# Layer 3's cross-attention weights loaded during layer 1's experts, and their token-free preparation moved into the head of layer 2's cross-attention

## The reference

```python
q_in = x @ Wq + (x @ q_down @ q_up) * alpha_q / 32
org_ctx, ipa_ctx = context[:, :end], context[:, end:]          # end = 12544 - 4
k_in = org_ctx @ Wk + (org_ctx @ k_down @ k_up) * alpha_k / 32
v_in = org_ctx @ Wv + (org_ctx @ v_down @ v_up) * alpha_v / 32
out = _attention(q_in, k_in, v_in)                              # 16 heads of 64
out = out + _attention(q_in, ipa_ctx @ Wk_ipa, ipa_ctx @ Wv_ipa)  # the last 4 tokens
return out @ Wo + bo + lora(out, o_down, o_up, o_alpha)
```

## Time and profile before

| | |
|---|---|
| median of 3 runs | 3099.08 us (3098.6 to 3107.48) |
| the profiled execution, own time | 3106.17 us |
| its span, first to last instruction | 3104.5 us |
| PE busy | 2802.7 us, 90% |
| DVE busy | 1799.1 us, 58% |
| mean granted TensorE clock | 0.914 of 2.4 GHz |
| x2, the streamed cross-attention of layer 2 | 1312.0 to 1641.6 us |
| L3_q, the first stage of x3 | 1741.6 to 1840.4 us |
| L_units, 112 units | from 1841.7 us |

### The profile page before, as it was taken

One profiled execution on the slowest core, in us unless ns is written; L12 is line 12 of the kernel. 1 busy time (PEld: TensorE's weight loads), 2 busy tenths in 40 slices (PEclk: granted clock), 3 DMA queues, 4 the chain that ended last, 5 costly groups with the idle time before them and its releaser, 6 DMA issues. The chain is left out here.

```text
span 3104.5 us, 65465 instructions
## 1 busy us (share of the span) xinstructions
PE 2802.7 (90%) x26651; PEld 2312.9 (75%) x26651; DVE 1799.1 (58%) x3184; ACT 1322.1 (43%) x2169; POOL 409.8 (13%) x579
## 2 busy tenths in 40 slices
PE   7999869996699984889995699999999999999968
PEld 6999837773267764747774269999999999999857
DVE  5666468884378844578863235555555555555433
ACT  4555437772067761247771004443334444443311
POOL 3444400011001000000000041202020202000000
PEclk9999979997689996979996659999999999999879
DMA  5889697656777721687736411010000100000026
GB/s 165 323 304 346 261 255 192 175 140 215 216 186 188 190 58 48 213 198 188 188 105 226 114 42 42 12 31 20 23 25 18 33 10 1 1 1 1 18 77 223
DMA packets 193632, 393.98 MB, mean 127 GB/s; under 512 B 30472, under 2 KB 161865, under 8 KB 182574
## 3 DMA queue, kind: packets, MB, share of 16 engines
q1 hardware_dynamic: 178525, 341.33, 37.9%
q10 hardware_dynamic: 14804, 48.39, 4.1%
HBM read 290.13 MB, written 99.52 MB: 126 GB/s over the span
## 5 line engine op out<-in xcount | busy, mean ns | idle before, releaser
L878 DVE TENSOR_REDUCE L_xattn_tops<-psum 128x1 f32<-128x896 f32 x672 | 704.7, 1084 | 177.2 <-PE psum L704 175.0
L801 ACT ACTIVATE L_xattn_probs<-psum 128x512 f32<-128x512 f32 x1176 | 612.7, 601 | 352.1 <-PE psum L717 349.7
L1882 DVE TENSOR_SCALAR_CACHE_REDUCE L_units_raw<-psum 128x448 f32<-128x448 f32 x448 | 277.3, 619 | 463.0 <-PE psum L1798 460.5
L1842 ACT ACTIVATE L_units_raw<-L_units_raw,L_units_negmax 128x896 f32<-128x896 f32 x224 | 221.7, 1037 | 593.2 <-DVE L_units_negmax L1892 593.2
L1818 PE MATMUL psum<-wide_tokens,L_units_high 128*128 128x386 f32 x1568 | 456.7, 358 | 1.4 <-DVE L_units_low L1901 1.4
L704 PE MATMUL psum<-L_xattn_keys,L_xattn_q_stack 96*128 96x448 bf16 (+1 forms) x1344 | 390.2, 374 | 57.6 <-DMA L_xattn_q_stack<-query_parts 22.2
L717 PEld LDWEIGHTS psum<-L_xattn_q_stack,L_xattn_keys 99*128 99x128 bf16 (+1 forms) x4704 | 308.4, 98 | 169.9 <-issue 76.8
L717 PE MATMUL psum<-L_xattn_q_stack,L_xattn_keys 99*128 99x128 bf16 (+1 forms) x4704 | 406.3, 222 | 6.0 <-POOL L_xattn_q_stack L850 2.2
L1819 PE MATMUL psum<-wide_tokens,L_units_low 128*128 128x194 f32 x1568 | 395.4, 252 | 0.0
L733 PE MATMUL psum<-L_xattn_probs,L_xattn_values 128*17 128x128 f32 x9408 | 333.6, 278 | 1.5 <-issue 1.5
L1818 PEld LDWEIGHTS psum<-wide_tokens,L_units_high 128*128 128x128 f32 x1568 | 294.7, 188 | 11.2 <-DVE L_units_low L1901 1.6
(11 more groups left out here) (497 smaller groups left out, 3737.0 us busy)
## 6 DMA issues: line engine op xcount, KB each, us to landing
key_parts<-proj_parts SPq DMA_DIRECT2D x84, 672.0 KB, 5.3
L_xattn_keys<-key_parts SPq DMA_DIRECT2D x252, 224.0 KB, 4.6
L_xattn_keys<-key_parts SPq DMA_DIRECT2D x252, 168.0 KB, 3.6
values_scratch<-held ACTq DMA_DIRECT2D x12, 1904.0 KB, 11.6
L_xattn_values<-values_scratch SPq DMA_DIRECT2D x45, 476.0 KB, 6.1
values_scratch<-proj_values ACTq DMA_DIRECT2D x9, 1904.0 KB, 9.1
L_ffn_w<-in_L_ffn_w SPq DMA_DIRECT2D x16, 1024.0 KB, 7.4
L_experts_w<-in_L_ffn_W SPq DMA_DIRECT2D x16, 1024.0 KB, 11.6
```

The source lines that it names most:

```text
L801: act.activation(group_probs(k), score_bank(k), ACT.Exp).then_inc(sem("probs"), 1)
L878: dve.tensor_reduce(tops[:, h % 2, 2 * c + w:2 * c + w + 1], top_slot(n), AX.XY, ALU.max)\
L1842: act.activation(half, half, ACT.Exp, bias=new).then_inc(sem("probs"), 1)
L1882: dve.tensor_scalar(raw[u % 2][:, s * SUB:s * SUB + width], bank(g, s % 2, 0, width), 0.0, None, ALU.add, ALU.max, accum_out=tops[:, h, s: ...
```

## The change

A new function loads six weights of layer 3 on SP at the end of f1, behind expert 7's `w2`. They go into buffers that exist from f1 on (`g.early`, `g.wv_a`, `g.wv_b`, `g.q_down`); `g.early` later serves for tiles of the last two stages as well.

```diff
+def layer3_weights(eng, g, a):
+    n, landed = "L3_xattn_", g.layer3.sem("weights")
+    eng.dma_start(g.wkT, a[n + "Wk_T"].rearrange("(i p) c -> p i c", p=128)).then_inc(landed, 16)
+    eng.dma_start(g.wv_a[:], a[n + "Wv"][0:128, :]).then_inc(landed, 16)
+    eng.dma_start(g.wv_b[:], a[n + "Wv"][128:C, :]).then_inc(landed, 16)
+    landed = g.layer3q.sem("weights")
+    eng.dma_start(g.q_down[:], a[n + "q_down"].rearrange("(k p) n -> p k n", p=128)).then_inc(landed, 16)
+    eng.dma_start(g.q_up, a[n + "q_up"]).then_inc(landed, 16)
+    eng.dma_start(g.wq3, a[n + "Wq"].rearrange("(k p) n -> p k n", p=128)).then_inc(landed, 16)
```

In `streamed_cross_attention`, for layer 2 alone (`prepares`), each engine gets work. The small operands are slices of `probs`, which is free until unit 0. On PE the first part stands behind the query's products and ahead of the wait for `stack`; the rest is called in the loop over units:

```diff
+                if prepares:
+                    pe.wait_ge(sem("low_rank"), 16 * 7)
+                    for i in range(IG):
+                        pe.matmul(bank(g, 4 + i // 2, i % 2 * C, i % 2 * C + C), k_up[:, i * 128:i * 128 + 128], k_downT,
+                                  start=True, stop=True, skip_group_check=True).then_inc(sem("wk_in_psum"), 1)
+                    for j in range(2):
+                        cols = slice(j * BANK, j * BANK + BANK)
+                        pe.matmul(bank(g, j), v_downT[:, 0:128], v_up[:, cols], start=True, stop=True)
+                        pe.matmul(bank(g, 2 + j)[0:C1, :], v_downT[:, 128:C], v_up[:, cols], start=True, stop=True)\
+                          .then_inc(sem("wv_in_psum"), 1)
+                    pe.wait_ge(sem("wv"), 4)
                 pe.wait_ge(sem("stack"), STACK)
...
                     if k == 0:
                         pe.wait_ge(sem("key_rows"), 16)
+                        if prepares:
+                            pe.wait_ge(sem("v_ipa"), 2)
...
+                def ipa_keys():
+                    pe.wait_ge(sem("ipa_loads"), 16 * 6)
+                    pe.wait_ge(sem("wk"), 4)
+                    for i in range(IG):
+                        cols, out = slice(i * 128, i * 128 + 128), bank(g, 4, i * IPA, i * IPA + IPA)
+                        pe.matmul(out, wk_ipa_a[:, cols], ipa_a, start=True, stop=False, skip_group_check=True)
+                        last = pe.matmul(out, wk_ipa_b[:, cols], ipa_b, start=False, stop=True, skip_group_check=True)
+                    last.then_inc(sem("k_ipa_in_psum"), 1)
+
+                def ipa_values(j):
+                    pe.wait_ge(sem("rep"), 2)
+                    cols, out = slice(j * BANK, j * BANK + BANK), bank(g, 5 + j)[0:H * IPA, :]
+                    pe.matmul(out, rep_a, wv_ipa_a[:, cols], start=True, stop=False)
+                    pe.matmul(out, rep_b, wv_ipa_b[:, cols], start=False, stop=True).then_inc(sem("v_ipa_in_psum"), 1)
...
                     ahead, now = v < NU, 0 <= u < NU
+                    if prepares and u == -5:
+                        ipa_keys()
+                    if prepares and u in (-4, -3):
+                        ipa_values(u + 4)
```

On ACT seven loads stand ahead of the wait for the split query, and six loads and three copies behind the first values, ahead of the exponentials:

```diff
+                    if prepares:
+                        for dst, name3 in ((k_downT, "k_down_T"), (k_up, "k_up"), (v_downT, "v_down_T"), (v_up, "v_up")):
+                            act.dma_start(dst, a[n3 + name3]).then_inc(sem("low_rank"), 16)
+                        for i, which in enumerate("qkv"):
+                            act.dma_start(g.alpha3[:, i:i + 1], row_view(a[f"{n3}{which}_alpha"], 0, 1))\
+                               .then_inc(sem("low_rank"), 16)
                     act.wait_ge(sem("qparts"), 1)
...
                     fill_values(act, 0, c, n)
+                if prepares:
+                    for dst, src in ((ipa_a, a["ctxT"][0:128, NK - IPA:NK]), (ipa_b, a["ctxT"][128:C, NK - IPA:NK]),
+                                     (wk_ipa_a, a[n3 + "Wk_ipa"][0:128, :]), (wk_ipa_b, a[n3 + "Wk_ipa"][128:C, :]),
+                                     (wv_ipa_a, a[n3 + "Wv_ipa"][0:128, :]), (wv_ipa_b, a[n3 + "Wv_ipa"][128:C, :])):
+                        act.dma_start(dst, src).then_inc(sem("ipa_loads"), 16)
+                    act.wait_ge(sem("k_ipa_in_psum"), 1)
+                    act.copy(g.k_ipa[:].rearrange("p i j -> p (i j)"), bank(g, 4, 0, IG * IPA)).then_inc(sem("k_ipa"), 1)
+                    for j in range(2):
+                        act.wait_ge(sem("v_ipa_in_psum"), j + 1)
+                        act.copy(g.v_ipa[:, j * BANK:j * BANK + BANK], bank(g, 5 + j)[0:H * IPA, :])\
+                           .then_inc(sem("v_ipa"), 1)
```

POOL waits for `ipa_loads` and repeats the last tokens for 16 heads in two copies (`rep`), ahead of `split(0)`; behind `place(0)` it masks `g.v_ipa` with two affine_selects. DVE, behind the split of the query (`qparts`) and ahead of the two memsets of the head, does this:

```diff
+                if prepares:
+                    dve.wait_ge(sem("low_rank"), 16 * 7)
+                    dve.wait_ge(sem("layer3_weights"), 16 * 3)
+                    link(dve.tensor_scalar(g.alpha3[:], g.alpha3[:], 1.0 / RANK, None, ALU.mult))
+                    for i in range(0, IG, 2):
+                        dve.wait_ge(sem("wk_in_psum"), i + 2)
+                        wk = g.wkT[:, i:i + 2, :].rearrange("p i c -> p (i c)")
+                        dve.scalar_tensor_tensor(out=wk, in0=bank(g, 4 + i // 2, 0, 2 * C), scalar=g.alpha3[:, 1:2], in1=wk,
+                                                 op0=ALU.mult, op1=ALU.add).then_inc(sem("wk"), 1)
+                    for j in range(2):
+                        cols = slice(j * BANK, j * BANK + BANK)
+                        dve.wait_ge(sem("wv_in_psum"), j + 1)
+                        dve.scalar_tensor_tensor(out=g.wv_a[:, cols], in0=bank(g, j), scalar=g.alpha3[:, 2:3],
+                                                 in1=g.wv_a[:, cols], op0=ALU.mult, op1=ALU.add).then_inc(sem("wv"), 1)
+                        dve.scalar_tensor_tensor(out=g.wv_b[:, cols], in0=bank(g, 2 + j)[0:C1, :],
+                                                 scalar=g.alpha3[0:C1, 2:3], in1=g.wv_b[:, cols], op0=ALU.mult,
+                                                 op1=ALU.add).then_inc(sem("wv"), 1)
```

In `absorbed_queries` the same work and all its loads are taken out: SP only loads chunk 0, ACT only computes the exponential, PE keeps the transposes, `q_down`, the query, the last tokens' scores, the product with `wkT` and the last tokens' output; POOL keeps the two memsets and the split of chunk 0. In the experts:

```diff
                 if shared:
                     load(E, E % 2, shared[0], shared[2], at=0)
+                if layer == 1:
+                    layer3_weights(sp, g, a)
...
-    ALL_W2 = w_up is None
+    ALL_W2 = False
```

More of the change, by code:

```diff
@@ L547, in streamed_cross_attention @@
     masked, biased = layer == 0, layer > 0
+    prepares = layer == 2
     FLOOR = -1e20 if masked else -3.4e38
@@ L582, in stage @@
                 st.adopt(g.ahead[layer])
+                if prepares:
+                    st.adopt(g.layer3)
                 q = st.sb("q", [128, DG, T])
@@ L852, in place, with mask_values @@
                         pool.wait_ge(sem("shifted"), 4 * h + i + 1)
+                def mask_values():
+                    v = g.v_ipa.rearrange("p (h d) -> p h d", h=H)
+                    pool.wait_ge(sem("v_ipa"), 2)
+                    link(pool.affine_select(out=v, in_=v, compare_op=ALU.is_ge, fill=0.0, base=0,
+                                            pattern=[[-IPA, H], [0, DH3]], channel_multiplier=1))
+                    link(pool.affine_select(out=v, in_=v, compare_op=ALU.is_ge, fill=0.0, base=IPA - 1,
+                                            pattern=[[IPA, H], [0, DH3]], channel_multiplier=-1))
+                if prepares:
+                    pool.wait_ge(sem("ipa_loads"), 16 * 6)
+                    for out, in_, parts in ((rep_a, ipa_a, 128), (rep_b, ipa_b, C1)):
+                        pool.tensor_copy(out.rearrange("p (h j) -> p h j", j=IPA),
+                                         in_.unsqueeze(1).to_broadcast([parts, H, IPA])).then_inc(sem("rep"), 1)
                 for h in range(H):
@@ L856, in _ @@
                     place(h)
+                    if prepares and h == 0:
+                        mask_values()
             @block.vector
@@ L1571, in _ @@
         def _(sp):
-            def load(dst, src, what):
-                sp.dma_start(dst, src).then_inc(sem(what), 16)
-            load(k_downT[:], a[n + "k_down_T"], "k_loads")
-            load(k_up[:], a[n + "k_up"], "k_loads")
-            for i, which in enumerate("qkv"):
-                load(alpha[:, i:i + 1], row_view(a[f"{n}{which}_alpha"], 0, 1), "k_loads")
-            load(wkT[:], a[n + "Wk_T"].rearrange("(i p) c -> p i c", p=128), "k_loads")
-            load(v_downT[:], a[n + "v_down_T"], "v_loads")
-            load(v_up[:], a[n + "v_up"], "v_loads")
-            load(g.wv_a[:], a[n + "Wv"][0:128, :], "v_loads")
-            load(g.wv_b[:], a[n + "Wv"][128:C, :], "v_loads")
             load_chunk(sp, g, a, 0, sem("chunk"))
@@ L1588, in _ @@
             norm_tensor(pe, g, st)
-            pe.wait_ge(sem("k_loads"), 16 * 6)
-            for i in range(IG):
-                if i >= 2:
-                    pe.wait_ge(sem("wk"), i - 1)
-                pe.matmul(bank(g, 1 + i % 2, 0, C), k_up[:, i * 128:i * 128 + 128], k_downT[:], start=True, stop=True)\
-                  .then_inc(sem("wk_in_psum"), 1)
-            pe.wait_ge(sem("q_loads"), 16 * 3)
+            pe.wait_ge(sem("layer3q_weights"), 16 * 3)
             pe.wait_ge(sem("xnT"), 1)
@@ L1600, in _ @@
             last.then_inc(sem("qd_in_psum"), 1)
-            pe.wait_ge(sem("v_loads"), 16 * 4)
-            for j in range(2):
```

(25 more changed lines are left out.)

93 lines of the change are left out of this document (18 added, 75 removed).

## The result

| kernel | median | range | to the kernel before, with 95% interval |
|---|---|---|---|
| before | 3098.6 us | 3093.0 to 3107.5, 9 runs | |
| changed | 3082.5 us | 3075.9 to 3092.6, 9 runs | 0.9953 (0.9940 to 0.9967) |
| changed, second job | 3085.1 us | 3080.2 to 3092.5, 12 runs | 0.9968 (0.9954 to 0.9982) |

What follows compares the result with a forecast made beforehand. PE was taken to bound the long loops, with waiting chains in the short stages between. Saving 46.4 us in L3_q and paying 22.6 in x2's head gives -23.8 us on the 3099.1 us median: 3075 us, range 3056 to 3088.

Steps and rivals of the forecast that it cites:

- the two terms of the sum: Whole kernel: 46.4 us saved in L3_q and 22.6 us paid in the head of x2, together -23.8 us.
- The forecast's own range: Whole kernel: 3067 to 3083 us, with the head costing 19 to 30 us and L3_q saving 45 to 47; forecast chance 63%.
- What L3_q saves: L3_q: query starts without waiting for weights, last tokens' keys and values are gone, scores start earlier: 46.4 us saved.
- The low-rank part: Head of x2: products for `wkT` and `Wv` outlast PE's old wait, up to 1328.23, by 5.7 us (4 to 9).
- The last tokens' work: Head of x2: `ipa_keys` loses 8.2 us and the two `ipa_values` 3.6 us each, together 15.4 us.
- The wait for the six loads: Head of x2: PE waits for the loads `ipa_keys` needs, issued by ACT behind the values: 1.5 us (0 to 6).
- a sign of being wrong: Clock above 0.50 in either chain, first top later than 25 us, or over 6 us wait for the last tokens' loads.
- Sum of the head: Head of x2: low-rank part 5.7, last tokens' part 15.4 and wait for loads 1.5, together 22.6 us paid.
- No price for f1, `w2` and POOL's split: Loads behind f1 cost 0; later `w2` in a2 costs 0 with 3 us to spare; L3_q's split hidden by 19 us.
- The clock at 0.50 in both chains: L3_q and head of x2: all prices taken at 1.2 GHz, as PE ran these matmuls at 0.50 for 80 us.
- the first rival: Clock rises in L3_q (3059 us), in the head of x2 (3064) or in both (3048); chance 16%.

Runs made afterwards that it cites:

- all three traces with the old order: The kernel before, traced twice, and w2_alone: L3_q took 100.1, 97.5 and 97.9 us, x2 340.6, 340.2 and 340.4 us.
- tokens_in_q: Changed kernel with the last tokens' loads and products back in L3_q, early weights and low-rank part kept in x2's head: 3077.3 us, 0.9939 to the kernel before.
- tokens_early: Changed kernel with the last tokens' six loads issued by SP between the keys of head 0 and head 1: 3074.7 us, 0.9940 to the kernel before.
- after_again: The changed kernel once more, unchanged, in a second job: 3085.1 us, 0.9968 to the kernel before.
- w2_alone: The kernel before with only the new place of w2 of layer 2's experts 4 to 7: 3095.2 us, 1.0002 to the kernel before.
- gaps_filled: Changed kernel with 12 useless 128x128 identity products filling PE's pauses in L3_q, 8 of them ahead of the transposes: 3063.5 us in one run.
- after: The changed kernel in its first job and first trace: 3082.5 us, 0.9953 to the kernel before.
- traffic: Changed kernel with four useless 1.2 MB DRAM copies issued by SP at the head of layer 2's expert stage: 3078.9 us in one run.
- sixty_dense: Changed kernel with 60 useless identity products ahead of L3_q's transposes instead of 8: 3085.4 us in one run.
- the tail runs: Changed kernel, last tokens' part in x2's last units: 3075.3 us; low-rank part there too: 3073.4 us; narrow key matmuls also spread over four units: 3081.7 us.

## Why the prediction was right, and where it was not

The sign and the stated range (3056 to 3088) hold, and the two terms of the sum come out within 6 us. The forecast's own range, 3067 to 3083, holds the first median at its edge and not the second. Term by term:

- **What L3_q saves, 46.4 us.** Up to the scores it was 46.6 (66.8 to 20.2 us after the stage's start): the chain was read rightly. The step that failed is "from there PE and DVE do the same work as before": that rest took 35.1 us instead of 33.2. 1.5 of the 1.9 us are one operation, below. From its start to its last operation the stage took 53.6 us, with 52 expected. Against all three traces with the old order the stage is 42 to 45 us shorter.
- **The low-rank part, 5.7 us.** The first top came 22.5 us after the start (22 predicted) and 6.3 later than before; its loads landed 8.0 us after the start, 7 predicted. At the end of x2 only 3.8 us of it were left (tokens_in_q). In that trace DVE's top windows start 6.0 us later than before up to the eighteenth, and 4.3 us later from the twenty-third on; between them the clock rises, some 47 us after the start, before the change some 44. So fewer of the first units run at 1.2 GHz, and that gives back most of the difference.
- **The last tokens' work, 15.4 us.** 11.7 by the difference of tokens_early and tokens_in_q. The gaps of DVE behind the first were 3.31 and 2.32 us, not 4 and 4: the clock rose in the second value product, the last `L786` taking 1.35 us where the one before took 1.97.
- **The wait for the six loads, 1.5 us (0 to 6).** This is the step that failed: 5.6 to 12.2 us in five traces, and four of them are over the 6 us that the prediction named as a sign of being wrong. PE came when expected (30.8 us after the start); the loads were late. The estimate gave ACT's queue half of the DMA engines, and half it got, but it took the rate of a stretch of 5 us, 321 GB/s. From the values' issue to the landing of the six the two queues together moved 236 GB/s (changed kernel; q10 is ACT's queue, with MB and share), and 207 in after_again:

```profile
DMA packets 2269, 4.69 MB, mean 236 GB/s; under 512 B 618, under 2 KB 1514, under 8 KB 2269
q1 hardware_dynamic: 669, 2.26, 50.9%
q10 hardware_dynamic: 1600, 2.43, 50.9%
```

  2.43 MB at half of 236 GB/s are 20.6 us instead of 15. The trace of before could have told: over the 21 us from the first top on it has 199 GB/s, at a full share.

```profile
1328.60:1350.00 21.40, 17.54 (x46) 3.61 (x45) 19.07 (x20) 1.09 (x2) 1.59 (x8) 0.50 1.03 199
```

  A range from one execution was too narrow as well. tokens_early, without the wait, is 4 to 13 us shorter in x2, of which up to 2.5 are the clock at x2's end.
- **Sum of the head, 22.6 us.** 20 to 28. It came out near by luck, because the two errors cancel: 6 us too much for the work, 4 to 11 too little for the wait.
- **No price for f1, `w2` and POOL's split**: f1 took 76.2 us; w2_alone shows no difference; the split ended 20.6 us ahead of the stage's last operation (19 predicted).
- **The clock at 0.50 in both chains**, and the first rival (a rise, 16%). It did not come about, and the reason given against it, that these very matmuls had run at 0.50 for 80 us, held: they did so again in the changed kernel. What it left out is the level at which they start. In gaps_filled the clock had risen before the query began, behind the useless products, and the query then kept it. By the Trainium skill (TensorE: Matmul & The Clock Gate, Part 1, The HAM clock gate) sustained activity releases the throttle, and for the useless products the trace agrees. It does not agree for the 37 us in the kernel before, nor in the heads, where PE was busy at 0.50 for 19 us in every trace.
- **The time.** 3075 was predicted, 3082.5 and 3085.1 were measured, and x2 and L3_q together account for 14 to 22 us in the three traces of the change against the three with the old order. The medians' 10 to 16 lie at the lower end. a3 and f3, which were not touched, take 133.4 to 134.9 us in the three old traces and 135.1 to 138.0 in the five with the changed placement of both parts in x2's head; some 3 us go there, and the clock is what differs. These are the first 10 us of a3, and 5 us of f3 from 121 us after a3's start, each before and in the changed kernel:

```profile
2971.06:2981.06 10.00, 7.51 (x49) 7.12 (x50) 3.01 (x8) 0.00 (x0) 1.00 (x3) 0.68 1.03 391
2936.20:2946.20 10.00, 7.52 (x41) 7.13 (x42) 2.10 (x6) 0.00 (x0) 1.00 (x3) 0.58 1.03 391
3092.06:3097.06 5.00, 5.00 (x33) 4.61 (x32) 1.81 (x3) 1.26 (x2) 0.00 (x0) 1.00 0.05 16
3057.20:3062.20 5.00, 5.00 (x25) 4.66 (x24) 0.71 (x2) 0.63 (x1) 0.00 (x0) 0.66 0.35 124
```

  a3 took 47.5, 47.6 and 48.7 us in the old traces and 49.1 to 49.7 in all others. f3 took 88.2 to 88.7 us in the four traces in which the clock fell once more there (after, after_again, traffic, sixty_dense) and 85.8 to 86.7 in the rest. What moves these moments stays open.

## What to carry to other kernels

Work moved ahead is free only where its new place has a pause on the same engine that is as long; two windows in flight hide almost nothing, and the loads that it needs come with it into a place that may be short of DMA. Of this change, moving the weights' loads and the low-rank part was worth 29 us of L3_q for under 4 us of x2, while the last tokens' part was worth 14 and cost 16 to 24: price each part by itself. Before a move is priced, look which clock its old and its new place have, read the DMA rate over a stretch as long as the loads will take, and take their landing times from more than one execution.

## What was not expected of the hardware

**DVE stood still for a POOL instruction.** One small product from SBUF to SBUF took 0.66 us before and 2.15 after, and 1.84 to 2.20 in the six other traces in which it met the same copy. Both of its inputs lie in SBUF, and it ends just when POOL's copy ends (changed kernel, timeline):

```profile
1778.30 2.43 POOL L1649 CAST wide_tokens<-wide_tok 128x2688 fp32r<-128x2688 f32 x1
...
1778.65 2.15 DVE L1755 TENSOR_TENSOR L_q_p<-L_q_p,L_q_total 128x64 f32<-128x64 f32 x1
...
1781.65 0.79 PE L1704 MATMUL psum<-L_q_qT,early 64*128 64x128 f32 x2 [2.07 <-DVE wide_q_low L1763]
```

The copies from PSUM behind it are not slowed. In the kernel before, this product met a copy of POOL that was near its end (1812.66 + 1.68 = 1814.34, and the product ended at 1814.4). In all fourteen traces it ends 0.07 to 0.08 us behind the POOL operation that was running when it started, whichever that was, so even its 0.66 us are in part a wait. The Trainium skill (SBUF — State Buffer, Who interferes with whom) has it so: a DVE operation with two SBUF inputs and a GpSimd operation that reads SBUF exclude each other, and the second waits for the whole of the first. Moving POOL's split earlier thus moved its long copy onto this product, and PE waited 2.07 us behind it.

**The clock has a memory.** The query does not raise it (15 us busy at 0.50) and does not lower it (8.4 us at 1.00). It fell in or just behind matmuls with 4 columns in five kernels (the tail runs, gaps_filled, sixty_dense), and in the 5 us before each fall PE had no pause longer than 0.4 us. Spread among other work it fell in the third of their four pieces. That these matmuls are the cause is argued from the place of the five falls; no run leaves them out of such a place alone. In one and the same kernel it rose at moments that made a2's expert stage 50.4 or 46.1 us long. What in PE's work raises or lowers it was not taken further apart.
